# Expert projections with 512 tokens streaming and experts summed in PSUM

## The reference

```python
x = hidden_states.reshape(n, c)
...
w = jax.nn.softmax(masked, axis=-1)                  # (n, 16), zero for experts not chosen
def moe_proj(p):
    y = jnp.einsum('nc,ech->neh', x, p)
    return jnp.einsum('ne,neh->nh', w, y)
q, k, v = moe_proj(q_proj), moe_proj(k_proj), moe_proj(v_proj)
scores = jnp.einsum('bth,bsh->bts', q, k) / sqrt(h)
attn = softmax(scores)
o = jnp.einsum('bts,bsh->bth', attn, v).reshape(n, h)
z = jnp.einsum('ne,nh->enh', w, o)
out = jnp.einsum('enh,ehc->nc', z, o_proj)
```

## Time and profile before

| what | us |
|---|---|
| median of 3 runs | 799.25 |
| lowest, highest | 798.65, 804.01 |
| the profiled execution | 805.03 |
| its span (first to last instruction) | 803.2 |
| busy in it: TensorE, VectorE, ScalarE, GpSimd | 688.1, 634.6, 444.7, 155.5 |
| projections to q, k, v (first product to last) | 521.1 to 660 |
| attention | 660 to 737 |
| output projection and last norm | 730 to 803 |

### The profile page before, as it was taken

The page is one execution under the profiler, slowest core; times in us unless marked ns, Lnnn a source line. Parts: engine busy times, 40 slices in busy tenths (PEclk is TensorE's granted clock), DMA queues, the critical chain, the costliest instruction groups (busy, mean ns, idle before and its releaser), DMA issues.

```text
span 803.2 us, 16661 instructions
## 1 busy us (share of the span) xinstructions
PE 688.1 (86%) x5878; PEld 440.5 (55%) x5878; DVE 634.6 (79%) x1148; ACT 444.7 (55%) x974; POOL 155.5 (19%) x287
## 2 busy tenths in 40 slices
PE   7599888888888888899954988499999998998883
PEld 4233333333333333335633766499999997996652
DVE  1688999999999999952574557889999994554996
ACT  3158999999999999984641356212111114454442
POOL 7300000000000000002431007601111122123563
PEclk9658999999999999999985589589999998999998
DMA  6811111111111110002546510000000000000000
GB/s 191 220 30 32 31 33 31 32 32 31 33 31 32 32 31 3 2 3 56 155 132 169 154 29 0 1 1 0 2 0 0 0 0 1 0 0 1 15 13 26
DMA packets 19329, 31.87 MB, mean 40 GB/s; under 512 B 4928, under 2 KB 12480, under 8 KB 17920
## 3 DMA queue, kind: packets, MB, share of 16 engines
q1 hardware_dynamic: 17920, 29.42, 14.0%
q0 software_dynamic: 1344, 1.58, 0.7%
HBM read 23.25 MB, written 7.34 MB: 38 GB/s over the span
## 4 chain that ended last, share of the span: by engine, by line
PE 53%; ACT 18%; issue 10%; DVE 9%; DMA 4%; POOL 3%; SPq 2%; DVEq 0%; POOLq 0%; ACTq 0%
ACT probs L1145 16%; PE ps_hi L728 13%; PE ps_lo L977 7%; PE ps_lo L979 7%; PE ps_lo L978 7%; PE ps_hi L742 4%; PE ps_hi L1037 3%; DVE mx L1440 2%; DVE probs L1722 2%; DMA q_rep<-mrow 2%; PE ps_hi L1028 1%; PE ps_hi L909 1%; PE ps_lo L874 1%; ACT mrow L1100 1%; PE ps_hi L789 1%
## 5 line engine op out<-in xcount | busy, mean ns | idle before, releaser
L1440 DVE TENSOR_REDUCE mx<-ps_lo 128x2 f32<-128x1024 f32 x256 | 306.2, 1224 | 11.2 <-PE ps_lo L705 8.3
L1145 ACT ACTIVATE probs<-ps_hi 128x512 f32<-128x512 f32 x512 | 277.9, 597 | 38.0 <-PE ps_hi L728 25.1
L742 PE MATMUL ps_hi<-probs,v_blk 128*32 128x256 f32 x2048 | 167.8, 400 | 5.8 <-ACT mrow L1100 5.6
L728 PE MATMUL ps_hi<-q,k 28*128 28x512 f32 x512 | 131.6, 507 | 27.6 <-ACT probs L1145 13.7
L705 PE MATMUL ps_lo<-k,q 26*128 26x512 f32 x512 | 134.9, 524 | 6.6 <-DVE mx L1440 4.2
L1656 DVE SCALAR_TENSOR_TENSOR tok_cur<-ps_lo,w_cur,tok_cur 128x384 f32<-128x384 f32 x240 | 127.5, 608 | 6.2 <-PE ps_lo L979 4.9
L728 PEld LDWEIGHTS ps_hi<-q,k 28*128 28x128 f32 x512 | 49.3, 186 | 140.4 <-ACT probs L1145 118.4
L977 PE MATMUL ps_lo<-w_hi,op_hi 128*128 128x384 f32 (+1 forms) x304 | 108.0, 355 | 20.0 <-DVEq L1617 10.0
L979 PE MATMUL ps_lo<-w_hi,op_lo 128*128 128x384 f32 (+1 forms) x304 | 105.3, 347 | 0.0
L978 PE MATMUL ps_lo<-w_lo,op_hi 128*128 128x384 f32 (+1 forms) x304 | 105.3, 346 | 0.0
L742 PEld LDWEIGHTS ps_hi<-probs,v_blk 128*32 128x32 f32 x2048 | 42.3, 109 | 72.1 <-ACT probs L1145 58.9
(11 more groups left out here) (224 smaller groups left out, 840.9 us busy)
## 6 DMA issues: line engine op xcount, KB each, us to landing
q<-q_parts SPq DMA_DIRECT2D x32, 192.0 KB
q_rep<-q_parts SPq DMA_DIRECT2D x8, 576.0 KB
k<-k_parts SPq DMA_DIRECT2D x32, 96.0 KB
k_rep<-k_parts SPq DMA_DIRECT2D x24, 96.0 KB
q_parts<-qk_hi SPq DMA_DIRECT2D x8, 256.0 KB, 4.3
q_parts<-qk_p SPq DMA_DIRECT2D x12, 128.0 KB, 3.2
xa<-in_L_attn_x SPq DMA_DIRECT2D x4, 256.0 KB, 3.6
q_parts<-qk_lo SPq DMA_DIRECT2D x4, 256.0 KB, 4.6
```

The lines of the kernel that those rows point to most:

```text
L728: mm = pe.matmul(bank(4 + (2 * n + a) % 3), k0[rows, k_at:k_at + P], q0[rows, h * QN:(h + 1) * QN], start=True, stop=True)
L742: mm = pe.matmul(o_bank()[32 * r:32 * r + 32, 0:OW], v_all[:, at:at + 32], probs0[:, n % P_RING, r * OW:(r + 1) * OW], start=(kb == 0), st ...
L1145: act.activation(probs0[:, n % P_RING, a * QN:(a + 1) * QN], bank(4 + (2 * n + a) % 3), ACT.Exp).then_inc(s0_free, 1)
L1440: dve.reduce_max(mx2[:, j % 2, :, i, kh], bank(2 * (m % 2), 2).rearrange("p (a n) -> p a n", a=2), AX_X).then_inc(max0_done, 1)
```

## The change

The expert weight is applied to the tokens before the product. For each expert and quad, TensorE copies the quad's 512 weights over all partitions (`pick_weights`: a 32-row stationary matrix of ones at the wanted rows, times the transposed weights; four experts in the four row strips, into four banks), VectorE multiplies the transposed tokens with it (`z_scaled`), ScalarE rounds (`z_first`), and GpSimd or, for every third expert, VectorE makes the rest (`z_second`). Then the expert's weights are stationary and z streams, 512 tokens at a time; all 16 experts add up in one PSUM bank for each of q, k and v. The results come transposed: q and k as the attention wants them, v is transposed back. The output projection works in the same way, three products for each expert and quad; its result is copied, transposed and added to the residual in PSUM, and the norm is the one of the other layers. The rings z_cur, z_hi, z_lo hold four experts. The weights are transposed twice (w_rt, and w_rt divided by the softmax sums). v's and q's handling per tile on GpSimd is gone. One constant of 128 x 512 is loaded more, early.

```diff
-YR = 4
+ZR = 4
+BLK = 3
+NZ = NQ * E
...
         def res_bank(n, q):
-            return bank(q if n == 1 else 4 + q)
+            return bank((4 + q, q, 4 + q, (4 + q) % 7)[n])
+        def second_by_dve(idx):
+            return idx % 3 == 2
+        def pick_bank(idx):
+            return bank((4 if idx < NZ else 0) + idx % QUAD)
+        def acc_bank(g, blk):
+            return bank((BLK * g + blk) % 4)
+        def out_bank(g):
+            return bank(4 + g)
```

On GpSimd:

```diff
+            for idx in range(2 * NZ):
+                if not second_by_dve(idx):
+                    z_second(idx)
+                q = (idx - NZ) // E - 1
+                if q >= 0 and idx % E == 9:
+                    root(3, q)
```

On TensorE; qkv_products is wait_second and `three` for q, k and v, out_products wait_second and one `three`, finish_rows the residual's add_rows and quad_products with ident_sb:

```diff
+            def first_weights(g):
+                pe.wait_ge(wr_set, g + 1)
+                if g:
+                    pe.wait_ge(wT_sb, g)
+                w_transposes(g, bank(3))
+            def pick_weights(n):
+                g, kq = n // QUAD % NQ, n % QUAD
+                pe.wait_ge(wT_sb, n // QUAD + 1)
+                if n:
+                    pe.wait_ge(z_set, QUAD * n)
+                for a in range(QUAD):
+                    rows = slice(STRIP * a, STRIP * (a + 1))
+                    pe.matmul(pick_bank(QUAD * n + a), pick_r[rows, kq * P:(kq + 1) * P],
+                              wT[rows, g * QN:(g + 1) * QN], start=True, stop=True).then_inc(bc_ps, 1)
+            def three(dst, at, idx, first, last):
+                hi, lo, u = w_hi[:, at:at + P], w_lo[:, at:at + P], idx % ZR
+                pe.matmul(dst, hi, z_hi[:, u, :], start=first, stop=False)
+                pe.matmul(dst, lo, z_hi[:, u, :], start=False, stop=False)
+                return pe.matmul(dst, hi, z_lo[:, u, :], start=False, stop=last)
+            first_weights(0)
+            pick_weights(0)
+            for idx in range(NZ):
+                if idx % QUAD == 2 and idx + QUAD < NZ:
+                    pick_weights(idx // QUAD + 1)
+                qkv_products(idx)
+                if idx in (1, 3, 5):
+                    first_weights((idx + 1) // 2)
...
+            for g in range(3):
+                v_transposes(g)
+            scores(0)
+            scores(1)
+            v_transposes(3)
+            probs_T(0)
+            for t in range(NT):
+                if t + 2 < NT:
+                    scores(t + 2)
+                if t == NT - 2:
+                    pe.wait_ge(p_set, NT - 1)
+                    for g in range(2):
+                        second_weights(g, bank(g))
+                outputs(t)
+                if t + 1 < NT:
+                    probs_T(t + 1)
...
+            pick_weights(NZ // QUAD)
+            for idx in range(NZ, 2 * NZ):
+                if idx % QUAD == 2 and idx + QUAD < 2 * NZ:
+                    pick_weights(idx // QUAD + 1)
+                out_products(idx)
+                if idx == NZ + 3:
+                    pe.wait_ge(o_sb, NT)
+                    for g in range(2, NQ):
+                        second_weights(g, bank(4 + g))
+                q = (idx - NZ) // E - 1
+                if q >= 0 and idx % E == 3:
+                    finish_rows(q)
+            pe.wait_ge(z_set, 2 * NZ)
+            finish_rows(NQ - 1)
```

On ScalarE:

```diff
+            def z_first(idx):
+                act.wait_ge(z_set, idx + 1)
+                if idx >= ZR:
+                    act.wait_ge(prod_done, idx - ZR + 1)
+                copy(z_hi[:, idx % ZR, :], z_cur[:, idx % ZR, :]).then_inc(zhi_set, 1)
...
+            for idx in range(NZ, 2 * NZ):
+                z_first(idx)
+                if idx == NZ + 7:
+                    for g in range(2, NQ):
+                        wT_copy(NQ + g, bank(4 + g))
+                q = (idx - NZ) // E - 1
+                if q >= 0 and idx % E == 2:
+                    outT_copy(q)
+                if q >= 0 and idx % E == 11:
+                    normalise(3, q, xb)
```

On VectorE:

```diff
+            def z_scaled(idx):
+                g = idx // E % NQ
+                dve.wait_ge(bc_ps, idx + 1)
+                if idx >= ZR:
+                    dve.wait_ge(zhi_set, idx - ZR + 1)
+                    wait_second(dve, idx - ZR)
+                dve.tensor_tensor(z_cur[:, idx % ZR, :], xT[:, g * QN:(g + 1) * QN], pick_bank(idx), ALU.mult).then_inc(
+                    z_set, 1)
+            def z_second(idx):
+                dve.wait_ge(zhi_set, idx + 1)
+                dve.tensor_tensor(z_lo[:, idx % ZR, :], z_cur[:, idx % ZR, :], z_hi[:, idx % ZR, :].bitcast(F32),
+                                  ALU.subtract).then_inc(zlo_dve, 1)
...
+            for idx in range(NZ, 2 * NZ):
+                if idx % E == 0:
+                    dve.wait_ge(o_sb, QUAD * (idx // E - NQ + 1))
+                z_scaled(idx)
+                if second_by_dve(idx - 1) and idx > NZ:
+                    z_second(idx - 1)
+                if idx == NZ + 1:
+                    divide(1)
+                q = (idx - NZ) // E - 1
+                if q >= 0 and idx % E == 7:
+                    stats(3, q, fin_ps)
+                if q >= 0 and idx % E == 10:
+                    shift(3, q)
```

More of the change, by code:

```diff
@@ new lines, in scores @@
+            def scores(t):
+                u, b = t % 2, t // KB
+                if t < 2:
+                    pe.wait_ge(acc_lo, 7 + t)
+                    pe.wait_ge(acc_v, 3 + t)
+                else:
+                    pe.wait_ge(p_set, t - 1)
+                q_at = slice(t * P, (t + 1) * P)
+                for i in range(2):
+                    k_at = slice(b * S + i * QN, b * S + (i + 1) * QN)
+                    pe.matmul(bank(2 * u + i), qT_hi[:, q_at], kT_hi[:, k_at], start=True, stop=False)
+                    pe.matmul(bank(2 * u + i), qT_hi[:, q_at], kT_lo[:, k_at], start=False, stop=False)
+                    mm = pe.matmul(bank(2 * u + i), qT_lo[:, q_at], kT_hi[:, k_at], start=False, stop=True)
+                mm.then_inc(sc_ps, 1)
@@ L1057, in _ @@
-            outputs(NT - 2, 0, NB - 1)
-            def group(pair, a, n):
-                for u in range(2):
-                    pe.wait_ge(acc_step, NT + 8 * (pair * 3 + n - 1))
-                    product(bank((2 * (3 * a + n - 1) + u) % 4), a, u, E * W3 + n * 4 * D, 4 * D).then_inc(z_ps, 1)
-            def first_group(pair, a):
-                pe.wait_ge(xc_set, NT + QUAD + 2 * pair + 2)
-                for u in range(2):
-                    pe.wait_ge(z0_sb, 2 * pair + u + 1)
-                    product(bank(4 + 2 * a + u), a, u, E * W3, 4 * D).then_inc(z0_ps, 1)
@@ L1073, in out_quad @@
-            def out_quad(q, begin, end):
-                for a in range(2):
-                    pair = 2 * q + a
-                    if not (begin and a == 0):
-                        group(pair, a, 1)
-                    if not (end and a == 1):
-                        first_group(pair + 1, 1 - a)
-                    group(pair, a, 2)
-                    group(pair, a, 3)
-            pe.wait_ge(xc_set, NT + QUAD + 2)
-            group(0, 0, 1)
-            probs_T(NT - 1, 1)
-            pe.wait_ge(pt_sb, 2 * NT + 2)
@@ L1267, in expert_quad @@
-            def expert_quad(i, end):
-                for a in range(2):
-                    pair = 2 * i + a
-                    act.wait_ge(y_ps, 2 * E * (pair + 1))
-                    for u in range(2):
-                        copy(op_hi[:, a, u, :], xT[:, bass.ds((2 * pair + 4 + u) % NT * P, P)])\
-                            .then_inc(op_hi_set, 1)
-                    if not (end and a == 1):
-                        first_expert(pair + 1, 1 - a)
-                    if not (end and a == 1):
-                        kq_copies(pair, a)
@@ new lines, in _, with p_exp @@
+            wT_copy(0, bank(3))
+            for idx in range(NZ):
+                z_first(idx)
+                if idx in (5, 7, 9):
+                    wT_copy((idx - 3) // 2, bank(3))
+                if idx >= E and idx % E == 2:
+                    qkv_copies(idx // E - 1)
+            qkv_copies(NQ - 1)
+            for g in range(2, NQ):
+                act.wait_ge(vt_ps, g + 1)
+                copy(v_tok[:, g * QN:(g + 1) * QN], bank(4 + g)).then_inc(vt_sb_act, 1)
+            def p_exp(t):
+                u = t % 2
@@ L1314, in o_copy @@
-            def o_copy(t, u):
-                act.wait_ge(o_ps, t + 3)
-                copy(oT_all[:, bass.ds(t * P, P)], bank(6 + u)[:, 0:P]).then_inc(o_sb, 1)
-            p_exp(0, 0)
-            kq_copies(NT // 2 - 1, 1)
-            p_exp(1, 1)
-            pT_copy(0, 0)
-            def attend(first, last):
-                with act.Fori(first, last) as i:
-                    for u in range(2):
-                        t = 2 * i + u
-                        o_copy(t, u)
-                        pT_copy(t + 1, 1 - u)
-                        p_exp(t + 2, u)
@@ new lines, in _, with outT_copy @@
+            p_exp(0)
+            p_exp(1)
+            pT_copy(0)
+            for t in range(NT):
+                if t == NT - 2:
```

(12 more changed lines are left out.)

571 lines of the change are left out of this document (193 added, 378 removed).

## The result

The changed kernel takes 856.35 us (median of 4 runs, 852.82 to 864.19) against 799.82 us (4 runs) before: 1.0675 times as long, interval 1.0617 to 1.0732 (the quotient of the two medians, 1.0707, lies inside it). Forecast were 846.4 us, 1.059 times. The profiled execution took 852.82 us, its span 850.9, 47.7 more than the span before.

The account below looks back on a forecast made before the run. TensorE bounds the q, k, v projections, the z chain's loop the output projection. Span 803.2 plus 9.6 (later start), 36.0 (output projection onward), 1.5 (half clock) and 0.1 gives 850.4; plus 1.8 less 5.8, 846.4 us; range 826 to 862.

Parts of the forecast that it names:

- Streaming, and the sums that go: q, k, v projections: TensorE binds; 576 products at 0.2275 take 131.0 us against 133.1; VectorE's 240 sums weren't the bound.
- Late start: q, k, v projections: all products need the weights, so the first comes at 530.2; 9.1 of the stage's +12.4 us.
- Half clock behind it: Start of q, k, v projections: 5.5 us at half speed after TensorE's idling, charged 2.7 us (0 to 3).
- Picks: q, k, v projections: four products copying weights over all partitions, 0.45 us a quad, 15 x 0.45 = 6.8 us.
- Attention: Expert attention: TensorE work per tile unchanged, start +0.3 us; output projection begins 9.6 us later, at 746.2.
- I keep the clock loss: Attention's start: TensorE idles about 2 us again, so the half clock stays; without it -3.2 us.
- The loop: Output projection: pick, z_scaled, z_first, rest, two products, next pick in series; mean 5.06 us a quad, 82.5 in all.
- the extras: Output projection, beside the loop: division, weight parts, three groups' copy, statistics, normalisation; 0 to 17.5 us, taken as 10.
- By that rule [...] it doesn't bind: Output projection: VectorE and GpSimd subtractions exclude each other; three experts need 3.29 us of shared path in 3.80 of loop.
- (1): Rival: z chain stays hidden in the output projection too, no slower than before; 797 us at the median; chance 0.11.
- (2): Rival: half clock all through the output projection, each quad 0.9 longer, +14.5, 861 us; chance 0.13.
- (3): Rival: loop binds, extras mostly beside it (3 not 10), picks 0.25 (3 less each projection); 833 us; chance 0.14.

Follow-up runs that it names:

- Cutting the loop: Changed kernel with only the first quad of picks in the output projection, 15 later quads left out, z_scaled rereading the first: 844.24 us, 1.0574.

## Why the prediction held

**Streaming, and the sums that go.** Products step 0.2275 us and TensorE is full, so 131.0 us of products held, and taking 240 sums off VectorE bought nothing in this stage, as forecast.

**Late start.** First product forecast at 530.2, measured 529.27. These 0.9 us are the execution's and not the forecast's: w_rt was done at 522.87 here and at 523.81 in the profile before, though the work up to it is the same. From there to the first product it took 6.40 us, and 6.4 were forecast. Half clock behind it lasts until 533.2, 3.9 us and not 5.5, a loss of 1.9 and not 2.7.

**Picks.** This term was mis-sized: 0.635 us a quad where 0.45 was taken, 15 x 0.19 = 2.8 us more. The row strips of the earlier trace rows gave the duration rightly (0.50), but that is not what a quad displaces. With the start 0.9 early and 0.8 less half clock the stage ends 1.0 late, at 673.38 (672.4). (The forecast's +12.4 counts from 660.0, the end of the last product before, and not from the 660.23 that stands beside it; its sum isn't touched, since the attention's 7.3 counts from there too.)

**Attention.** The step "I keep the clock loss" was wrong: TensorE idled 1.78 us before L1001, and the clock stayed at 1.00. The third tile's scores started 7.3 us after the projections (7.6); from there to the last tile's (733.66) it takes 52.9 us and not 55.7, which is the clock's part; and the first pick came at 744.45, 1.9 before the forecast 746.3 although the stage began 1.0 late. That is 2.9 less, the 2.8 us that filling the same gap gave the kernel before.

**Output projection.** The loop held. The three steps in a row at full clock with nothing beside them are 5.45, 4.86 and 4.84, mean 5.05, against 5.47, 4.86, 4.86 and 5.06; the few other steps without a group's end in them are less close, 5.27 (mostly at half clock), 5.50 and 5.22. First product 3.33 after the pick (3.4). From the first pick to the end of the products 96.4 us against 82.5 + 10 + 1.5 = 94.0; the 2.4 are in the extras and the half clock, 13.9 for both and not 11.5. The two steps behind a group's end sum to 12.55, 12.62 and 12.05 against 10.1 for two clean ones, 6.9 us for the three groups of the 15.6 that they would cost all in a row; the first two steps (division, second weight transposes, half clock) are 3.0 over, and one step at half clock (7.15) 2.1. End: 7.3 after the last product, and 2.75 behind the normalisation, both as forecast.

**What the forecast's reason left out.** Cutting the loop showed that it is the nearest limit, not the only one: a second, GpSimd and VectorE excluding each other on the rests, stands at 4.2 us a quad, close behind the loop's 5.06. "By that rule [...] it doesn't bind" was right for this kernel, and would have misled anyone who planned to mend it by the order alone.

**Sum.** The span came out at 850.9 against 850.4: -1.9 in the start of the output projection and +2.4 in it. That is closer than the steps deserve: picks +2.8, the router's earlier end -0.9, half clock behind it -0.8, attention -2.9, output projection +2.4. That they cancel to half a microsecond is luck; the waits and the loop are not. The 10 us between 846.4 and the median of 856.35 are not the mechanism's: the profiled execution before lay 5.8 us above its median, which the forecast took off, and the one after lies 3.5 below its own. Measured again beside other runs of the kernel before, the ratio is 1.0628 (1.0548 to 1.0707), which holds the forecast 1.059; the first interval, 1.0617 to 1.0732, lies just above it.

**The rivals.** (1), the chain hidden, is excluded by the wait rows; it holds in the q, k, v stage alone. (2), half clock all through, came in three stretches only, some 17 of 96 us; what the forecast held against it, that the same stage ran at full clock before, is so up to 780 us, while the window from 780 to 800 shows 0.91. (3) fell with picks at 0.635 and 13.9 us of extras and half clock.

## What to carry to other kernels

A producer chain over several engines that is fed by TensorE itself needs as much TensorE work behind its first instruction as the chain is long: the same four links were free behind 4.1 us of products and kept TensorE waiting for some 1.7 of every 5.05 us behind 1.37. When a chain like that is found, look for the second limit before moving it, and take its price from undisturbed rounds: cutting the loop gave 10 us and not 30, because two engines that hold each other up stood right behind at 4.2 us a quad, and because the norm, copies and half clock beside the loop stayed. And work taken off an engine is worth nothing where that engine wasn't last, as with VectorE's sums in the projections to q, k and v; the work put in its place can cost all the same.

## What the runs showed of the hardware

Four products in the four row strips, 32 rows and 512 columns each, add 0.21 to 0.23 us when doubled, as much as one product of full height; a lone set among full-height products costs 0.635, and 0.4 of it is the change to strips and back. A subtraction of two SBUF operands, 128 x 512, takes 0.69 us on VectorE and 1.29 on GpSimd, and 1.28 and 1.5 when they meet. TensorE's granted clock stayed at 1.00 after 1.78 us of idling before L1001 in the changed kernel, and fell to 0.50 between 666.6 and 666.8 us in the kernel before, about 1 us after idling of 1.96 us at the same place had ended, and about 0.4 us after idling of 2.83 us before 747.78. In the output projection it fell twice more, near 785.8 and 809.6 us, 0.5 and 1.0 us after idling of 1.68 and 1.93 us before the picks at 785.25 and 808.64, where the two steps at a group's end lie. So the length of one idle stretch doesn't decide it (1.68 with a fall, 1.78 without), and the runs don't say more exactly what does.
